# Attention and expert kernel: query copies masked out of PSUM, pattern tiles exchanged by DMA, a split opening, values as fp32 row tiles

## What is computed

```
n = layernorm(x)
q_n, q, k, k_m, v = split(n @ W_prep + b_prep)      # 8 heads of 32, windows of 8x8
score  = bias + q_n . pat_n + q . k + k_m . pat_m   # 64 x 64 per window and head
score  = (score - mean) / sqrt(var(ddof=1) + 1e-5)  # no softmax
x      = x + (score @ v) @ W_fin + b_fin
t      = x + top2_of_8_experts(layernorm(x))        # gelu MLP 64 -> 256 -> 64
```

## Time and profile before

| | us |
|---|---|
| median of 3 runs (199.69 to 200.60) | 200.33 |
| the profiled execution | 199.29 |
| its span, first to last instruction | 197.5 |
| TensorE busy | 162.4 (82%) |
| VectorE busy | 125.8 (64%) |
| ScalarE busy | 115.2 (58%) |
| POOL busy | 34.5 (17%) |
| the DMA queue of SP, share of 16 engines | 22.9% |
| mean granted TensorE clock | 0.991 |

### The profile page before, as it was taken

One profiled execution on the slowest core, in us unless ns is written; L12 is line 12 of the kernel. 1 busy time (PEld: TensorE's weight loads), 2 busy tenths in 40 slices (PEclk: granted clock), 3 DMA queues, 4 the chain that ended last, 5 costly groups with the idle time before them and its releaser, 6 DMA issues.

```text
span 197.5 us, 6111 instructions
## 1 busy us (share of the span) xinstructions
PE 162.4 (82%) x2504; PEld 96.9 (49%) x2504; DVE 125.8 (64%) x365; ACT 115.2 (58%) x236; POOL 34.5 (17%) x82
## 2 busy tenths in 40 slices
PE   0049969695688689978996986999999999999992
PEld 0025438464455589765975942445244633432321
DVE  6894647999545734483896386159793757484353
ACT  6742677977353247958566457752766455767440
POOL 7999000000140000000060070000150006000000
PEclk9999999999789999999999999999999999999999
DMA  5840396159720000000000000500042003300510
...
DMA packets 8892, 12.37 MB, mean 63 GB/s; under 512 B 2960, under 2 KB 5528, under 8 KB 8864
## 3 DMA queue, kind: packets, MB, share of 16 engines
q1 hardware_dynamic: 8832, 11.96, 22.9%
...
## 4 chain that ended last, share of the span: by engine, by line
PE 59%; DVE 18%; ACT 10%; issue 8%; DMA 2%; POOL 1%; SPq 1%; ACTq 0%; DVEq 0%; POOLq 0%
PE PSUM L662 12%; PE PSUM L673 11%; PE PSUM L532 7%; DVE TN L814 5%; PE PSUM L560 4%; PE PSUM L725 4%; ACT HR L883 3%; PE PSUM L613 3%; PE PSUM L623 3%; PE PSUM L640 2%; DVE XN L1034 2%; PE PSUM L520 2%; DVE TM L1081 2%; DMA XR<-in_x 2%; PE PSUM L651 2%
## 5 line engine op out<-in xcount | busy, mean ns | idle before, releaser
L883 ACT ACTIVATE HR<-PSUM,B1P 128x512 f32<-128x512 f32 x64 | 38.8, 688 | 22.2 <-PE PSUM L662 22.2
L662 PE MATMUL PSUM<-X,W1G 64*128 64x512 f32 x128 | 31.8, 615 | 0.0
L673 PE MATMUL PSUM<-HR,W2s 128*64 128x512 f32 x128 | 30.8, 604 | 0.0
L532 PE MATMUL PSUM<-XS,WS 64*128 64x512 f32 x64 | 19.0, 732 | 2.0 <-ACT KT L858 2.0
L466 POOL TENSOR_SCALAR RZ<-MV 128x4 f32<-128x4 f32 x4 | 0.9, 230 | 94.3 <-DVE MV L1010 94.3
L662 PEld LDWEIGHTS PSUM<-X,W1G 64*128 64x128 f32 x128 | 11.0, 186 | 11.7 <-issue 11.0
L673 PEld LDWEIGHTS PSUM<-HR,W2s 128*64 128x64 f32 x128 | 7.9, 136 | 17.7 <-issue 16.8
L939 ACT ACTIVATE BV<-PSUM 64x256 f32<-64x256 f32 x32 | 12.2, 383 | 6.0 <-PE PSUM L593 5.8
L814 DVE COPY TN<-PSUM 64x256 f32<-64x256 f32 x32 | 13.6, 426 | 2.7 <-PE PSUM L560 2.0
L1172 DVE TENSOR_TENSOR SR<-PSUM,TN 128x512 f32<-128x512 f32 x16 | 10.3, 686 | 7.9 <-PE PSUM L623 7.8
L871 ACT ACTIVATE TN<-PSUM 64x256 f32<-64x256 f32 x32 | 12.1, 377 | 5.2 <-PE PSUM L560 4.7
...
## 6 DMA issues: line engine op xcount, KB each, us to landing
...
```

The costliest lines, as they stand in the source:

```text
L532: return nc.tensor.matmul(ps[:, :], WS[g * C:g * C + C, col:col + P], moving, start=True, stop=True)
L662: end(nc.tensor.matmul(ps[:, :], W1G[k, 2 * ep + d, :], X2[k, j * 512:j * 512 + 512], start=True, stop=True), "h", n)
L673: m = nc.tensor.matmul(ps[d * C:d * C + C, :], W2s[:, 2 * (2 * ep + d) + c, :], HR[(4 * u + 2 * d + c) % 8][:, :], start=(c == 0), stop=(c ...
L883: A(HR[n % 8][:, :], PS[b][:, :], ACT.Gelu, bias=B1P[:, col:col + 1]).then_inc(bank_drained[b], 1)
```

## The change

- BD's copies are written straight from PSUM: a projection is multiplied by a per-partition 0/1 mask MK (even or odd heads) and a masked bias BPM is added, once per parity (`spread`). No STG, no zeroing, no moves. In chunk 3 ScalarE makes all of them. Chunk 1's projections go between the patterns.
- A pattern tile is copied whole, one instruction each, even tiles on ScalarE, odd on VectorE. Windows then lie on the wrong partitions, and SP exchanges halves of TN per quad with three dependent DMAs (`swap`); SR waits for its quad. W1R is loaded behind the first exchange.
- Opening in two halves, the root as a POOL power, transposes, projections and keys in the order HEAD, and 16 matmuls on IDN ahead of them. PN moves from ScalarE to POOL. SP loads REL's first part ahead of BP.
- XC is computed by POOL (halving sums over a window, then a subtraction), plain fp32. `values` makes two fp32 matmuls, on rows 0 to 63 and 64 to 127, into banks 6 and 7; it now follows `score` (in step 0 the order is values, b1, score). `ss` and `y` come behind `o`, ScalarE's SSB behind OR.

```diff
+HEAD += [("k",) + key_tile(i) for i in range(4)] + [("bd", 0, 2), ("bd", 0, 3)]
+HEAD += [("k",) + key_tile(i) for i in range(4, 8)]
+
+
 def stage_b():
 
-    units = lambda c, numbers: [(True, c, i) for i in numbers]
-    chunk = lambda c: [(False, c, n) for n in range(4)]
-    order = units(0, [0]) + chunk(2) + units(0, [1, 2, 3]) + chunk(3) + units(1, range(4))
-    order += units(2, [0]) + chunk(4) + units(2, [1, 2, 3]) + units(3, [0]) + chunk(5) + units(3, [1, 2, 3])
+    order = []
+    for c in range(4):
+        order += [(True, c, 0)] + [(False, c + 1, n) for n in (0, 1)]
+        order += [(True, c, 1)] + [(False, c + 1, n) for n in (2, 3)] + [(True, c, 2)]
+        if c == 3:
+            order += [(False, 5, n) for n in range(4)]
+        order += [(True, c, 3)]
     return order
 
 
 def make_plan():
-
-    plan = [(("xt", j), (0, 1, 2, 7)[j], 1) for j in range(NG)]
...
         p = t // 2
-        s = [(("v", p), 6, 1), (("score", p), 0, 1)] + at("ss", 7) + at("on", 6, 0) + at("lg", 6) + at("y", 7)
+        v = [(("v", p, k), 6 + k, 1) for k in range(2)]
+        s = [(("score", p), 0, 1)] + v
         if p:
             s += [(("o", p - 1), 4, 1)]
         else:
-            s += [(("b1", c), 4 + c, 1) for c in range(2)]
+            s = v + [(("b1", c), 4 + c, 1) for c in range(2)] + s[:1]
...
-            for c in range(4):
-                for n in range(4):
-                    sp.wait_ge(*drained("bd", c, n))
-                sp.wait_ge(bd_zeroed[c // 2], ZEROS[c // 2])
-                for h in range(4):
-                    r = slice(HD * h, HD * h + HD)
-                    sp.dma_start(BD[c][r, :, h % 2, :], STG[c % 2][r, :, :]).then_inc(bd_in[c % 2], 16)
...
+            quads = TN[:, :, :, :].rearrange("p (t w) h o -> p t w (h o)", w=2)
+
+            def swap(j):
+
+                t = slice(4 * j, 4 * j + 4)
+                keep = SWAP[(j // 2) * C:(j // 2) * C + C, j % 2, :, :]
+                sp.dma_start(keep, quads[C:P, t, 0, :]).then_inc(swapped[j], 16)
+                sp.wait_ge(swapped[j], 16)
+                sp.dma_start(quads[C:P, t, 0, :], quads[0:C, t, 1, :]).then_inc(swapped[j], 16)
+                sp.wait_ge(swapped[j], 32)
+                sp.dma_start(quads[0:C, t, 1, :], keep).then_inc(swapped[j], 16)
+                sp.wait_ge(swapped[j], 48)
+
+            for tile in range(12, 16):
+                sp.wait_ge(*drained("t", tile))
+            swap(0)
             for d in range(2):
                 sp.dma_start(W1R[d * C:d * C + C, :, :], W1[:, :, d * P:d * P + P]).then_inc(w1r_in, 16)
+            for j in range(1, NG):
+                swap(j)
+
...
-            for lo in range(2048, 8192, 1024):
-                pool.memset(zero(0, lo, lo + 1024), 0.0).then_inc(bd_zeroed[0], 1)
-            for lo in range(6144, 8192, 1024):
-                pool.memset(zero(1, lo, lo + 1024), 0.0).then_inc(bd_zeroed[1], 1)
-            step(pool.memset(CEN[:, :], 0.0))
-            step(pool.memset(CEN[0:C, 0:C], -1.0 / WT))
...
+            step(pool.memset(MK[:, :], 0.0))
+            for q in range(4):
+                step(pool.memset(MK[HD * q:HD * q + HD, q % 2:q % 2 + 1], 1.0))
+            for half in range(2):
+                cols = slice(8 * half, 8 * half + 8)
+                pool.wait_ge(ve_ready, half + 1)
+                pool.tensor_tensor(RS[:, cols], VE[:, cols], NHALF[:, 0:8], ALU.pow).then_inc(rs_ready, 1)
+
+            pool.wait_ge(bp_in, 16)
+            for m, kind in enumerate((QN, KM)):
+                last = pool.tensor_tensor(BPM[:, :, m, :],
+                                          BP[:, 2 * kind:2 * kind + 2].unsqueeze(1).to_broadcast([P, 2, 2]),
+                                          MK[:, :].unsqueeze(2).to_broadcast([P, 2, 2]), ALU.mult)
+            last.then_inc(bpm_ready, 1)
+            pool.wait_ge(reln_in, 16)
+            for oj in range(WH):
+                src = REL[:, 0, :, ::-1].rearrange("p g (y c) -> p g y c", c=SIDE)
+                last = pool.tensor_copy(PN[:, :, oj, :, :], src[:, :, :, WH - 1 - oj:2 * WH - 1 - oj])
+            last.then_inc(pn_ready, 1)
...
+
+            for j in range(NG):
+                pool.wait_ge(*drained("xt", j))
+            part = XC[:, 0:NW * WT // 2].rearrange("p (w o) -> p w o", w=NW)
+            step(pool.tensor_tensor(part, XS[:, :, 0:WT // 2], XS[:, :, WT // 2:], ALU.add))
+            size = WT // 4
+            while size:
+                step(pool.tensor_tensor(part[:, :, 0:size], part[:, :, 0:size], part[:, :, size:2 * size], ALU.add))
+                size //= 2
+            step(pool.tensor_scalar(XM[:, :], part[:, :, 0], -1.0 / WT, None, ALU.mult))
+            pool.tensor_tensor(XC[:, :].rearrange("p (w o) -> p w o", o=WT), XS[:, :, :],
+                               XM[:, :].unsqueeze(2).to_broadcast([P, NW, WT]), ALU.add).then_inc(xc_ready, 1)
...
-                    pe.wait_ge(*moved(c))
+                    for n in range(4):
+                        pe.wait_ge(*drained("bd", c, n))
                 last = [None, None]
                 ps = [begin("t", 2 * unit + r) for r in range(2)]
                 for u in range(8):
...
+            pe.wait_ge(consts_ready, 1)
+            for _ in range(16):
+                nc.tensor.matmul(PS[3][:, 0:P], IDN[:, :], IDN[:, :], start=True, stop=True)
+            for use in HEAD:
+                if use[0] == "xt":
+                    turned(use[1])
...
             def values(p):
 
-                ps = begin("v", p)
                 for k in range(2):
-                    lo, cols = (2 * p + k) * P, slice(256 * k, 256 * k + 256)
-                    nc.tensor.matmul(ps[:, cols], XC[:, lo:lo + P], WVH[:, :], start=True, stop=False)
-                    m = nc.tensor.matmul(ps[:, cols], XC[:, lo:lo + P], WVL[:, :], start=False, stop=True)
-                end(m, "v", p)
+                    lo, rows = (2 * p + k) * P, slice(k * C, k * C + C)
+                    ps = begin("v", p, k)
+                    end(nc.tensor.matmul(ps[:, 0:256], XC[rows, lo:lo + P], WV[rows, :], start=True, stop=True), "v", p, k)
...
-        def stage(engine, add, c, n):
+        def query(act, n, c):
 
             s, g = divmod(n, 2)
-            if c >= 4:
-                engine.wait_ge(*filled("t", 7))
-            elif c >= 2:
-                engine.wait_ge(*moved(c - 2))
+            act.wait_ge(*filled("t", 7))
+            act.wait_ge(*filled("bd", c, n))
+            lo = 1024 * (c % 2) + 512 * s
+            nc.scalar.activation(QP[:, g, lo:lo + 512], PS[4 + n][:, :], ACT.Identity,
+                                 bias=BP[:, 2 * Q + g:2 * Q + g + 1]).then_inc(bank_drained[4 + n], 1)
+
+        def spread(engine, masked, c, n):
+
+            s, g = divmod(n, 2)
             engine.wait_ge(*filled("bd", c, n))
-            bias = BP[:, 2 * KINDS[c] + g:2 * KINDS[c] + g + 1]
-            if KINDS[c] == Q:
-                lo = 1024 * (c % 2) + 512 * s
-                last = add(QP[:, g, lo:lo + 512], PS[4 + n][:, :], bias)
-            else:
-                last = add(token_order(c, STG[c % 2][:, g, :])[:, :, 16 * s:16 * s + 16],
-                           PS[4 + n][:, :].rearrange("p (w o) -> p o w", w=16), bias)
+            kind = 0 if KINDS[c] == QN else 1
+            src = PS[4 + n][:, :].rearrange("p (w o) -> p o w", w=16)
+            for h in range(2):
+                dst = BD[c][:, g, h, :].rearrange("p (o w) -> p o w", w=NW)[:, :, 16 * s:16 * s + 16]
+                last = masked(dst, src, MK[:, h:h + 1], BPM[:, h, kind, g:g + 1])
             last.then_inc(bank_drained[4 + n], 1)
 
-        def move_tn(engine, copy, tile, g):
+        def move_tn(engine, copy, tile):
 
...
-            o0 = 8 * unit
             engine.wait_ge(*filled("t", tile))
-            for w in range(2):
-                src = PS[tile % 4][g * C:g * C + C, :].rearrange("p (o s t w) -> p w s t o", o=8, s=2, w=2)[:, w]
-                dst = TN[w * C:w * C + C, :, 2 * r:2 * r + 2, g, o0:o0 + 8].rearrange("p t s o -> p s t o")
-                last = copy(dst, src)
-            last.then_inc(bank_drained[tile % 4], 1)
+            src = PS[tile % 4][:, :].rearrange("p (o s w) -> p s w o", o=8, s=2)
+            dst = TN[:, :, 2 * r:2 * r + 2, 8 * unit:8 * unit + 8].rearrange("p w s o -> p s w o")
+            copy(dst, src).then_inc(bank_drained[tile % 4], 1)
...
+            act.wait_ge(bpm_ready, 1)
+            for use in HEAD:
+                if use[0] == "bd" and use[2] % 2 == 0:
+                    spread(act, shift_masked, 0, use[2])
+                elif use[0] == "k" and use[1] == 0:
...
             for tile, c, i in stage_b():
                 if not tile:
-                    if c >= 4 or i % 2 == 0:
-                        stage(act, act_spread, c, i)
+                    if c >= 4:
+                        query(act, i, c)
+                    elif c == 3 or i % 2 == 0:
+                        spread(act, shift_masked, c, i)
```

(32 more changed lines are left out.)

265 lines of the change are left out of this document (99 added, 166 removed).

## The result

The changed kernel takes 188.61 us (median of four runs, 186.28 to 188.95) against 200.01 us for the kernel before on the same chip: a ratio of 0.9407, with a 95% interval of 0.9323 to 0.9491. It is faster, by 11.4 us where 19 were forecast, and inside the range. In some executions the clock is lower and the time longer whatever the kernel; the ratios leave these out, and where too few others remain there is no ratio. The profiled execution took 188.37 us, its span 186.6.

What follows compares the result with a forecast made beforehand. It took a chain mostly on TensorE (59%) as the bound: first scores 48.2 + attention 47.4 + clock 1.0 + unchanged rest 81.5 = 178.1 us of span, 179.9 executed, so 181 forecast; range 173 to 191.

Steps and rivals of the forecast that it cites:

- Opening: Kernel start to first pattern matmul: statistics and root in halves, ending in ScalarE's and VectorE's passes, 19.0 us instead of 32.2.
- Pattern stage: First pattern to first scores: 29.2 us, with VectorE's and ScalarE's PSUM passes as the bound and patterns done at 44.6.
- 64 matmul halves of a pattern in 1.16, four of these and a little: Pattern stage: TensorE's work per chunk, claimed to lie below VectorE's 5.7 us in chunks 0 and 1.
- W1R as the last wait: End of pattern stage: b1 waits for W1R, loaded behind the exchange, until 46.2; the last 3.6 us before first scores.
- Exchange: Pattern stage and attention: three dependent DMAs per quad at 3.3 us each, bounds 2.6 and 6.1; later quads hidden.
- Both rivals that made it long: Exchange steps: becoming the chain, slower kernel, 203 at 6.1 us a step, chance 0.04; or 4.5 to 5, about 188, 0.12.
- POOL: Pattern stage: POOL's copies, adds, centring (10.4 us) and memsets end by 36, wanted at 44, so hidden.
- That rival: Pattern stage: POOL's operations take 1.6 times as long, BV is ready at 52 and pair 0 waits; about 188, chance 0.10.
- Attention: First scores to first expert matmul: the new order makes 47.4 us instead of 46.4.
- 0.3 a pair, a gain of 2.2: Attention: the values' two fp32 matmuls run side by side in two banks, 0.3 instead of 0.58 us a pair.
- Clock: Ahead of b1: TensorE's idle of nearly 3 us lowers its clock, costing 1.0 us, bounds 0 and 2.
- The forecast case: Whole kernel: a time of 176 to 186 us, chance 0.64.

Runs made afterwards that it cites:

- e1: The changed kernel without the 16 warm-up matmuls on IDN at the start; ratio to the kernel before 0.941.
- e8: The changed kernel with every second pattern matmul left out and the others on twice the columns; ratio to the kernel before 0.9265.
- e7: The changed kernel with attention in the order of before and chunk 3's last projected tile spread by VectorE instead of ScalarE; median 188.41 us, no ratio.
- e2: The changed kernel without the twelve exchange DMAs and SR's waits on them; ratio to the kernel before 0.9373.
- e4: The changed kernel with projections of chunks 1 to 5 on 256 of their 512 columns; ratio to the kernel before 0.9303.
- e6: The changed kernel with each of the values' matmuls issued twice into the same columns; median 194.14 us.
- e5: The changed kernel with only the values of pairs 1 to 7 put back ahead of the scores; ratio to the kernel before 0.9354.
- e11: The changed kernel with values and b1 in their old places and chunk 3's last tile spread by VectorE; attention 51.11 us, no ratio given.

## Why the prediction was right, and where it was wrong

**Opening: right.** 19.0 forecast, 18.38 measured. The POOL power of 8 columns, taken as 1.8 between bounds of 1.05 and 2.1, took 1.67 and 1.81: columns count. The chain ends, as said, in ScalarE's passes (KT at 17.55). Costing the warm-up at 0 was a miss of 1.0 us (e1): "TensorE has nothing else before 9" is true, but without the warm-up its transposes and first projections, from then to 13 us, run at half speed.

**Pattern stage: wrong by 6.7 us, and this is the miss of the sum.** The failing step is "64 matmul halves of a pattern in 1.16, four of these and a little", and with it "VectorE per chunk 5.7 us, above TensorE's". The "little" is a chunk's four projections, eight records in two groups of 1.06: 2.1 us. So TensorE needs 4 x 1.09 + 2.1 = 6.5 us a chunk, above VectorE's 5.7 (5.9 with masked writes at 806 ns). The earlier trace rows had fifteen projection records of the kernel before in 5.86 us, and the stage's own took 1.99 us for eight; the forecast had them at hand. The timeline shows the chunks starting at 18.38, 25.10, 32.88 and 41.30, patterns ending at 51.50:

| chunk | forecast | after | e8 |
|---|---|---|---|
| 0 | 5.7 | 6.72 | 6.61 |
| 1 | 5.8 | 7.78 | 6.60 |
| 2 | 6.5 | 8.42 | 8.01 |
| 3 | 7.6 | 10.20 | 8.43 |
| sum | 25.6 | 33.12 | 29.65 |

The last column separates the errors. The patterns took 7.5 us more than forecast, of which 0.8 came back behind them (2.8 to the first scores, forecast 3.6). Of the 7.5, e8 takes 3.5 away: that is the supply of instructions (with 1.0 for the faster units), which the prediction did not have at all, and which stood in the trace of before as the 2.26 us stall in the middle of a unit. It had read that stall as a wait for BD's transfers. What e8 keeps is 4.0 us. In chunks 0, 1 and 3 (0.9, 0.8 and 0.8) that is mostly the projections; chunk 3 has four more of them, eight records in 1.92 us, for the query's next chunks. In chunk 2 the 1.5 us are ScalarE's: TensorE waits 1.85 us there for its last masked write, of which e7 gets 0.9 back with one tile moved to VectorE. The forecast had priced these writes at 0.6 to 0.685 each, and they took 0.775.

**W1R as the last wait: wrong.** The exchange started at 33.62, not 31.0, so W1R was issued at 43.78 and, 4.3 us a transfer in median as forecast, was there at 49.0. `b1` came at 52.2, behind patterns and values. From the exchange's start to the landing its length was 15.4 us, as forecast (15.2); that `b1` would wait for it fell with the pattern stage's other error, since the patterns, 6.9 us late, cover it.

**Exchange: right.** 3.3 us a step forecast, 3.2 to 3.6 in quad 0, 3.1 to 3.2 to landing in median; only the first step of quad 1, issued behind W1R's two transfers, took 5.8. The others end at about 57, 67 and 76. Both rivals that made it long fall: e2 takes it away and gains nothing that can be told. The rule that a transfer over 64 partitions reaches half of the ports (the Trainium skill, SBUF — State Buffer, Door 1) gave an estimate of 3.3, and the trace's 3.1 to 3.2 agrees better with it than with the 2.6 of the other fit, which the Trainium skill (DMA: Bandwidth & Descriptors, Anatomy of one DMA) gives for DMAs on POOL's path, where these go out from SP. Pieces of 1 KB could make a transfer longer too; no run separates the two.

**POOL: right.** Its list ended at 34.2, forecast 36. The addition to XR took 2.36 us (2.33 before), the centring 2.38, 3.35 and 3.62, with its small step 9.9 in all where 10.4 was forecast, beside a busy VectorE. (By the forecast's own rate its elements come to 9.3, not 10.4.) That rival falls.

**Attention: 47.4 forecast, 50.75 measured, 3.3 of error.** The mechanism of the order was right: pair 2's `st` came 6.7 us behind its score (6.8 forecast), pairs 2 and 3 took 11.76 (11.3), pairs 4 and 5 13.75 (13.2). (The forecast's pairs add up to 47.6, not 47.4.) At full clock, in e4, the same attention takes 49.66, so 1.1 of the 3.3 is the clock. The failing term of the rest is the values: "0.3 a pair, a gain of 2.2" was 0.63, no gain but 0.4 of loss. Side by side was right, as the starts under e6 show. Wrong was the price of the matmul itself: the forecast gave a plain fp32 matmul the time of one float32r record of before, 0.15 us, and it takes two records of 0.21. The kernel before had this price in its projections, plain fp32 on row tiles too: eight records of 512 columns in 1.99 us, so four of 256 in about 0.5. In e6 another 0.43 us of values lengthened pairs 2, 4 and 5 by as much and pair 3 by nothing; so the 0.33 that the forecast missed makes 1.0 in these four, all that they are over it (25.5 against 24.5). The other 1.3 us lie in pairs 0, 1, 6 and 7 and stay open. The timeline of the changed kernel in pair 2:

```profile
61.36 1.09 PE L633 MATMUL PSUM<-IDN,TM 128*128 128x128 f32 x8
62.38 0.91 PE L643 MATMUL PSUM<-QP,KT 32*64 32x64 f32 x64
63.23 0.70 PE L614 MATMUL PSUM<-WV,XC 64*128 64x256 f32 x4
...
68.05 0.63 PE L726 MATMUL PSUM<-IDN,SSB 128*128 128x128 f32 x4 [1.30 <-ACT SSB L927]
```

**Clock: a drop came, at another place.** The 1.0 us was put down to an idle before `b1`, which wasn't there. It came in pair 6, behind a wait of 2.28 us for ScalarE's ONT copy:

```profile
94.49 1.09 PE L735 MATMUL PSUM<-IDN,ON 128*128 128x128 f32 x4 [2.28 <-ACT ONT L905]
...
96.00:98.00 2.00, 2.00 (x12) 1.64 (x11) 1.26 (x7) 0.73 (x2) 0.00 (x0) 0.57 0.03 8
```

At 0.57 it is at its 1.2 GHz level for most of the window. What that costs can be read from e4, whose attention is the same program: its pairs 0 to 5 agree with the changed kernel's within 0.02 us, it waits as long for ONT (2.29 us), and its clock stays at 1.00:

```profile
93.05 0.63 PE L738 MATMUL PSUM<-IDN,ON 128*128 128x128 f32 x4 [2.29 <-ACT ONT L908]
...
96.00:98.00 2.00, 2.00 (x88) 1.60 (x88) 1.80 (x8) 0.47 (x2) 0.00 (x0) 1.00 0.01 4
```

From the end of this wait to the first expert matmul e4 takes 9.46 us (93.05 to 102.51) and the changed kernel 10.55 (94.49 to 105.04). So the drop costs 1.1 us, close to the 1.0 forecast for another place: the size was right by luck. The one run of the changed kernel with a granted clock of 1.00 throughout took 186.28 us, 2.1 less than the next; the rest of that difference is open. Why the clock falls behind one such wait and not behind the other is not shown either: e5 has TensorE busy 2.28 of the 4 us from 88 to 92 and a clock of 1.00 behind it, e11 1.93 of 4 and then 0.50.

**The sum.** -0.6 + 6.7 + 2.4 (attention with the clock's 1.0) is the 8.5 us between 178.1 and the span of 186.6. The forecast case (176 to 186) failed by 2.6 us, and none of the rivals was what happened, so that 188.6 lies within 173 to 191 is in part luck: each was priced on the new parts (exchange, POOL, masked writes), while most of the error lay in TensorE's own old work, which the change had only moved, and in the supply of its instructions.
